# Last Fourier layer: the remaining field loads held back until the projected spectrum is back, and its small transfers split over two queues

## What is computed

```python
for i in range(L):                                   # L = 4
    x1 = _fourier_layer(v, W1, W2)                   # 12 x 12 modes, low and high rows
    x2 = jnp.einsum('bcxy,cd->bdxy', v, w_w[i]) + w_b[i][None, :, None, None]
    v = x1 + x2
    mean, var = jnp.mean(v, axis=(0, 2, 3), ...), jnp.var(v, axis=(0, 2, 3), ...)
    v = (v - mean) * jax.lax.rsqrt(var + BN_EPS)
    v = v * bn_g[i][None, :, None, None] + bn_b[i][None, :, None, None]
    if i < L - 1:
        v = jax.nn.relu(v)
out = jnp.einsum('bcxy,cu->bxyu', v, q_w) + q_b
h = jnp.squeeze(out)                                 # then tokens: attention, experts
```

## Time and profile before

| | us |
|---|---|
| median of 3 runs | 3424.24 |
| lowest and highest of them | 3412.07, 3430.98 |
| the profiled execution | 3428.21 |
| its span | 3426.4 |
| granted clock of TensorE over the span | 0.885 |

### The profile page before, as it was taken

One profiled execution on the slowest core, in us unless ns is written; L12 is line 12 of the kernel. 1 busy time (PEld: TensorE's weight loads), 2 busy tenths in 40 slices (PEclk: granted clock), 3 DMA queues, 4 the chain that ended last, 5 costly groups with the idle time before them and its releaser, 6 DMA issues. The chain is left out here.

```text
span 3426.4 us, 104381 instructions
## 1 busy us (share of the span) xinstructions
PE 2785.7 (81%) x45316; PEld 1470.8 (43%) x45316; DVE 2139.4 (62%) x3133; ACT 1389.1 (41%) x2280; POOL 607.9 (18%) x758
## 2 busy tenths in 40 slices
PE   0389999987999999789999975833578762999999
PEld 0145555554555555345555532211266650333333
DVE  2667777775687777667777763016466754555555
ACT  1245555554555555535555542001011110566665
POOL 0002333110133311003332110000144430000000
PEclk7689999998999999989999997976777766999999
DMA  5037666653988787378777853971122202567775
GB/s 161 10 79 171 146 141 148 142 127 107 275 262 254 236 255 229 103 229 261 246 245 248 254 185 145 415 219 37 49 61 69 64 20 60 95 119 120 119 121 90
DMA packets 243994, 541.26 MB, mean 158 GB/s; under 512 B 77856, under 2 KB 124704, under 8 KB 229952
## 3 DMA queue, kind: packets, MB, share of 16 engines
q1 hardware_dynamic: 234320, 529.04, 56.4%
q10 hardware_dynamic: 9264, 6.11, 0.9%
HBM read 320.28 MB, written 214.78 MB: 156 GB/s over the span
## 5 line engine op out<-in xcount | busy, mean ns | idle before, releaser
L794 ACT ACTIVATE p_v<-p_ps,k_scale_bias 128x1024 f32<-128x1024 f32 x384 | 445.9, 1201 | 642.9 <-PE p_ps L903 642.7
L663 DVE STREAM_TRANSPOSE p_t<-p_ps 128x1024 f32<-128x1024 f32 x192 | 361.9, 1957 | 308.3 <-PE p_ps L656 307.9
L778 POOL COPY k_xm<-p_sp 64x288 f32<-64x288 f32 x384 | 268.3, 699 | 1556.6 <-DVE p_sp L301 1539.9
L903 PEld LDWEIGHTS p_ps<-k_idfty,p_t 64*128 64x128 f32 x6144 | 397.8, 204 | 183.2 <-issue 183.2
L801 ACT ACTIVATE p_ps<-p_ps 128x1024 f32<-128x1024 f32 x384 | 388.4, 1011 | 165.3 <-PE p_ps L919 165.2
L903 PE MATMUL p_ps<-k_idfty,p_t 64*128 64x128 f32 x6144 | 438.7, 296 | 14.9 <-issue 14.9
L291 DVE STREAM_TRANSPOSE p_vt<-p_v 128x1024 f32<-128x1024 f32 x384 | 447.1, 1202 | 0.0
L2043 DVE TENSOR_TENSOR x_ht<-x_ht,x_mask 128x384 f32<-128x384 f32 x512 | 268.5, 555 | 246.9 <-ACT x_ht L2017 244.7
L2017 ACT ACTIVATE x_ht<-x_ph,x_b 128x384 f32<-128x384 f32 x576 | 303.0, 577 | 196.0 <-PE x_ph L2064 196.0
L894 PE MATMUL p_ps<-p_v,k_wbd 32*32 32x512 f32 x4096 | 304.8, 608 | 25.9 <-issue 14.0
L2064 PE MATMUL x_ph<-x_et,x_w 64*128 64x384 f32 x1152 | 266.3, 540 | 35.0 <-DMA x_b<-in_L_ffn_b1p_dram 33.8
(11 more groups left out here) (298 smaller groups left out, 3093.4 us busy)
## 6 DMA issues: line engine op xcount, KB each, us to landing
field<-p_v SPq DMA_DIRECT2D x768, 256.0 KB, 4.6
p_v<-field SPq DMA_DIRECT2D x64, 2048.0 KB
x_mask<-expert_weights SPq DMA_DIRECT2D x32, 1536.0 KB, 13.9
l_v<-field SPq DMA_DIRECT2D x16, 2048.0 KB, 25.8
k_xm<-field SPq DMA_DIRECT2D x12, 2048.0 KB, 24.7
k_mixw<-in_L_tok_fw_dram SPq DMA_DIRECT2D x16, 1152.0 KB, 9.7
at_cf<-state_coefficients SPq DMA_DIRECT2D x32, 384.0 KB
k_mixw<-field SPq DMA_DIRECT2D x4, 2048.0 KB, 24.6
```

The costliest lines, as they stand in the source:

```text
L663: return nc.vector.transpose(st[:, q].rearrange("p x c -> p c x"), ps[:, 2 * q:2 * q + 2, :].rearrange("p j (m c) -> p c j m", c=C))
L778: nc.gpsimd.tensor_copy(view[64 * k:64 * k + 64, :, j, :, G * i:G * i + G], sp[64 * j:64 * j + 64, :, :, 16 * k:16 * k + M1].rearrange("p ...
L794: nc.scalar.activation(field[:, 2 * q:2 * q + 2, CH * half:CH * half + CH], ps[:, e, 2 * q:2 * q + 2, :], ACT.Relu, bias=bias, scale=scale ...
L903: ins = nc.tensor.matmul(ps[:, e, 2 * q + h, col:col + 128], lines, K["idfty"][rows, :], start=False, stop=True, skip_group_check=True)
```

## The change

Four things change, all in `last_phase`.

- Two helpers, `store_projected(eng, k)` and `load_projected(eng, j)`, hold the two loops of the first round trip. ACT now issues two of the four stores and four of the eight loads; SP issues the other two and four. Each of the two queues waits for all four stores (`pj_out`, 64) before it issues its loads.
- On SP, the transfers of the first round trip come ahead of blocks 5 to 8. SP first waits for `pj_ready` and `pj_ready_v`.
- On SP, blocks 5 and later also wait for `pj_in`, 128, which is all eight loads of the first round trip.
- The number of own buffers has a name (`OWN` = 4) in place of the literal, and `arrived` lists two more semaphores, which are not reached with `NV` = 9.

The second round trip (`projected_rows`) is not touched: it stays on ACT's queue, in the same form.

```diff
+        def store_projected(eng, k):
+            for t in range(2 * k, 2 * k + 2):
+                cols = slice(3 * B * (t % 2), 3 * B * (t % 2) + 3 * B)
+                eng.dma_start(project[k][:, :, cols], pj[C * t:C * t + 4, :].rearrange("p (x m) -> p x m", x=M1)).then_inc(s.pj_out, 16)
+
+        def load_projected(eng, j):
+            src = project.rearrange("k (j r) x m -> k j r x m", j=2)
+            for r in range(2):
+                for k in range(2):
+                    at = 64 * j + KX * r + M1 * k
+                    eng.dma_start(sj[at:at + M1, :], src[k, j, r]).then_inc(s.pj_in, 16)
...
             eng.wait_ge(s.mix_done, NB)
-            load(4)
+            load(OWN)
+            eng.wait_ge(s.pj_ready, 5)
+            eng.wait_ge(s.pj_ready_v, 4)
+            store_projected(eng, 1)
+            eng.wait_ge(s.pj_out, 64)
+            load_projected(eng, 1)
             eng.wait_ge(s.pj_done, 9)
-            for k in range(5, n):
+            eng.wait_ge(s.pj_in, 128)
+            for k in range(OWN + 1, n):
...
             act.wait_ge(s.pj_ready, 5)
             act.wait_ge(s.pj_ready_v, 4)
-            for t in range(4):
-                cols = slice(3 * B * (t % 2), 3 * B * (t % 2) + 3 * B)
-                act.dma_start(project[t // 2][:, :, cols], pj[C * t:C * t + 4, :].rearrange("p (x m) -> p x m", x=M1)).then_inc(s.pj_out, 16)
+            store_projected(act, 0)
             act.wait_ge(s.pj_out, 64)
-            src = project.rearrange("k (j r) x m -> k j r x m", j=2)
-            for j in range(2):
-                for r in range(2):
-                    for k in range(2):
-                        at = 64 * j + KX * r + M1 * k
-                        act.dma_start(sj[at:at + M1, :], src[k, j, r]).then_inc(s.pj_in, 16)
+            load_projected(act, 0)
```

More of the change, by code:

```diff
@@ L978, in last_phase @@
     B = G * n
-    NV = 9
+    OWN, NV = 4, 9
     scale, bias = scale_bias
@@ L986, in last_phase @@
         w_sp, qs = sb("wsp", [P, C]), sb("qs", [P, 4])
-        own, scratch = sb("v", [P, 4, PX]), sb("j", [P, 4 * CH + P])
+        own, scratch = sb("v", [P, OWN, PX]), sb("j", [P, 4 * CH + P])
         ps = ctx.enter_context(nc.psum_tensor("l_ps", [P, 8, CH], F32))
@@ L993, in last_phase @@
         xf = K["xm"]
-        v = [own[:, k] for k in range(4)] + [spare[:, 0:PX]] + [xf[:, PX * k:PX * k + PX] for k in range(4)]
-        sy, hb = xf[:, 4 * PX:4 * PX + 16 * B], v[5]
+        v = [own[:, k] for k in range(OWN)] + [spare[:, 0:PX]] + [xf[:, PX * k:PX * k + PX] for k in range(4)]
+        sy, hb = xf[:, 4 * PX:4 * PX + 16 * B], v[OWN + 1]
         lx, ly, w_px = L["last_x"], L["last_y"], L["last_px"]
@@ L999, in arrived @@
         def arrived(k):
-            return (s.u_in0, s.u_in1, s.u_in2, s.u_in3, s.u_in4, s.u_in5, s.u_in6, s.u_in7, s.u_in8)[k % NV], 16 * (k // NV + 1)
+            return (s.u_in0, s.u_in1, s.u_in2, s.u_in3, s.u_in4, s.u_in5, s.u_in6, s.u_in7, s.u_in8, s.y_in0, s.y_in1)[k % NV], 16 * (k // NV + 1)
         def lines(k):
@@ L1016, in load @@
                 eng.dma_start(v[k % NV], V[order[k]]).then_inc(arrived(k)[0], 16)
-            for k in range(4):
+            for k in range(OWN):
                 load(k)
```

## The result

The changed kernel takes 3448.6 us (median of 6 runs, 3442.33 to 3460.44). The kernel before, run beside it again, takes 3430.09 us (median of 6, 3412.07 to 3442.46). The ratio is 1.0058, with a 95% interval of 1.003 to 1.0085: some 20 us **slower**, between 10 and 29. The forecast was 10 us slower, 3434, counted from a median of 3424.24 that three more runs moved to 3430.09.

The account below looks back on a forecast made before the run. DMA bounds the block stream, and the phase ends a fixed time after the last landing: 2109.2 + 88.5 + 14.5 + 57.2 = 2269.4, 9.8 us later, so 3424.2 + 9.8 = 3434 us; range 3412 to 3449.

Parts of the forecast that it names:

- the reads going by turns: Second round trip: each 512-byte read waits for one 16 KB block packet, 128 reads an engine.
- PE's wait: Ahead of the spectrum rows, PE waits 35 to 45 us for the second round trip's reads.
- the dry engines: Before block 21's data, DMA has no block to load for some 17 us, from T + 86.8.
- T: Time when PE has the first round trip's data, forecast at 2109.2 instead of 2130.9.
- (a): First round trip without blocks beside it: PE has its data at 2109.2, 21.7 us earlier.
- The upper bound of 2116: Latest T forecast for the first round trip, if its stores don't speed up at all.
- The rival of a late T: First round trip stays 25 us, its four engines being slow; 3454 us; chance 0.13 together with the slow clock.
- (d): Second round trip's reads go by turns with block loads; PE goes on at T + 88.5.
- (e): Spectrum rows and seventh pair after PE's wait: 14.5 us to block 21's issue, then 57.2 for eleven blocks.
- The rival of a slow clock: Half clock through spectrum rows, seventh and eighth pair: 13 us more, 3447; chance 0.13 together with a later T.
- not starved: Second round trip's reads done before T + 50, blocks without a gap: 6.1 us earlier, 3418; chance 0.25.
- The change doesn't do what it says: First round trip stays 25 us, T near 2130, 20 us later than forecast: 3454; chance 0.13 together with the slow clock.

Follow-up runs that it names:

- hold_alone: The kernel before plus only the wait of blocks 5 and later for all loads of the first round trip; 3456.01 us, ratio 1.008 to the kernel before.
- row_stores: The changed kernel with each row of a first-round-trip store as one piece of 18 KB; 3453.26 us, ratio 1.0068 to the kernel before.
- half_reads: The changed kernel with four of the eight reads of the second round trip left out; 3426.91 us, ratio 0.9997 to the kernel before.

## Why the prediction was right and wrong

The mechanism was right in each of its steps: the hold, the reads going by turns, PE's wait, the dry engines. What failed is its size, about half of the measured one in the medians (9.8 us against 18.5). Summed as the prediction did, from the first store's issue: 8.2 (T) + 88.5 + 14.5 + 57.2 = 168.4 forecast; 13.3 + 94.9 + 16.7 + 57.6 = 182.5 measured. The 14 us lie in three mis-sized terms. For the first of them, the packets of the stores in the changed kernel, 2092.79 to 2102.66:

```profile
q1 hardware_dynamic: 104, 0.15, 10.5%
q10 hardware_dynamic: 104, 0.15, 7.5%
```

That is 18% of 16 engines' 9.87 us, 28.4 us, for 192 packets of data: 0.15 us each.

- **(a), the round trip, 5.1 us.** T was forecast 8.2 us after the first issue and is 13.3. The step that failed is the price of a store packet: 0.076 us, from the burst behind the blocks. The stores alone are back after 9.87 us, not 5, and a packet took 0.15 us, twice the price. The burst was the tail of transfers long under way; why a packet was cheaper there is open. The upper bound of 2116 held it (2114.3 in the old positions), but I took the value near the low end. `hold_alone` and `row_stores` show that it was neither the second queue nor the packet count. The rival of a late T had said that these stores are slow by themselves; they are, but by 5 us and not by 20.
- **(d), the starving, 6.4 us, the largest.** PE went on at T + 94.9 (2201.0), forecast T + 88.5. The turns were priced with the lone read's 0.055 us. In the stream a 16 KB packet came each 0.70 us instead of 0.61, so a read cost its turn 0.09 us and a block took 5.6 us instead of 4.88 + 0.44. The engines were full to T + 89.9 (2196), forecast T + 86.8, some 3 us; the rest is the tail, 5.0 us with DMA at a share of 0.48 where 1.5 were forecast. The reads were issued when forecast, at T + 15.6.
- **(e), the restart, 2.2 us.** From PE's going on to the issue of block 21 it took 16.7 us, forecast 14.5. After 44.2 us of idling the spectrum rows ran at a granted clock of 0.50, the lower of the two levels (1.2 GHz), throughout: 6.8 us instead of 4.0 at 0.92. The clock stayed at 0.50 into the seventh pair, up to 2213, and was at 1.00 from 2214 on (0.72 over the 9.9 us). The rival of a slow clock had the mechanism, but a sixth of its price was paid.
- Eleven blocks took 57.6 us from issue to last landing, forecast 57.2. The time behind the last block grew by only 0.8 us.

On the rivals: *not starved*, which is also where the Trainium skill's rule of turns by whole packets of several descriptors led, did not happen: PE went on at T + 94.9, not before T + 75. `half_reads` comes close to what that case looks like, with PE going on at T + 65 and no dry engines. *The change doesn't do what it says* didn't either: the wait shrank by 16.6 us, from 30.6 to 14.0.

On the chances: 0.21 stood for slower by over 0.5%, and the measured ratio of 1.0058 is there, just. The median of 3448.6 lies just under the range's upper end, 3449, and that is luck in part: the end was made from some spread and a cold clock, priced at 12 us there and 13 in the rival's own sum, that cost 2. Of the 14.6 us between forecast and median, 6 are the later median of the kernel before; the rest is a loss of 18.5 us where 9.8 were forecast. All three missed terms erred to the same side: a rate from traffic's tail was taken for a lone transfer, a lone packet's time for one in traffic, and a warm stretch for a cold one. The range was made of whole cases and left little for that.

## What to carry to other kernels

When a wait is shortened, ask what used the idle time it made: here a second small transfer ran in the hole of the first one. In this case small packets in one queue beside a stream of 16 KB packets in another went at the stream's pace, about one for one, so their time was their number per engine times the big packet's (0.61 to 0.70 us), at 512 and at 1536 bytes alike. In the stream's own queue, or in a gap that held them, they cost under 10 us. Such a delay was free as long as released blocks kept the engines busy (15 us) and cost its time beyond (44 us), so find that edge before moving a transfer towards it.

## What the runs showed of the hardware

- With two queues full on the same engines, 512-byte reads advanced once per 0.68 us and 16 KB packets once per 0.70 us an engine; alone the same reads were through 9 us after their first issue, in traffic PE could go on 79 us after it (2121.72 to 2201.0).
- The Trainium skill, DMA: Bandwidth & Descriptors, section Queues, rings and completion order, puts the turn at a whole packet of several descriptors. In this case one row of the profile stands for one 512-byte piece, and the turn held about one such piece (74 against 71 in 50 us). If such a piece is a descriptor, the measurement differs from the page; how pieces are grouped into packets no run here shows.
- Four stores from four rows each, 288 KB in all, took 8.8 to 12.7 us with nothing beside them, in pieces of 1536 bytes or of 18 KB. At the stream's 430 GB/s block loads move as much in 0.7 us.
- Issuing took longer in traffic too: the eight reads took 35.22 us to issue in the changed kernel and 3.41 us before. In `half_reads`, at the same place and in the same traffic, four reads took 1.71 us, so the delay seems to begin behind the first four.
